# FFN 2's down product as fp32r halves, in the leaky gate's bank, with new orders of the last layers

## What is computed

```python
x = x + L1_ffn(LSTM(x, cond))      # int8-like activations, ternary weights, depthwise conv over time, SiLU
x = x + L2_ffn(RNN(x, cond))
x = x + L3_ffn(leaky(cond, x))

def _L2_ffn_ref(x, W1, b1, W2, b2):
    h = jnp.einsum('bsd,fd->bsf', x, _ternary(W1)) + b1          # 128 -> 512
    h = jax.nn.gelu(h, approximate=False)
    out = jnp.einsum('bsf,df->bsd', h, _ternary(W2)) + b2        # 512 -> 128
    return out

# L3 conditioning, a recurrence over time on the output of layer 2:
gate = jax.nn.sigmoid(h @ Wh.T + z_t @ Wz.T + b)
h_new = jnp.tanh(h * leak + gate * z_t)
```

## Time and profile before

| | |
|---|---|
| Time, median of 3 | 554.75 us (554.6 to 555.09) |
| Profiled execution, its own time | 554.63 us |
| Its span | 553.3 us |
| Granted TensorE clock | 1.0 of full speed |
| PE busy over the span | 540.1 us (98%) |
| DVE busy | 425.7 us (77%) |
| ACT busy | 380.6 us (69%) |
| POOL busy | 197.8 us (36%) |

### The profile page before, as it was taken

How to read it: one execution, slowest core, us unless ns; L and a number is a source line. 1 busy time by engine, 2 the same in 40 slices (tenths; PEclk the granted TensorE clock), 3 DMA queues, 4 the chain that set the end, 5 groups by cost and what they waited for, 6 DMA issues and landing times.

```text
span 553.3 us, 10078 instructions
## 1 busy us (share of the span) xinstructions
PE 540.1 (98%) x3341; PEld 468.0 (85%) x3341; DVE 425.7 (77%) x1026; ACT 380.6 (69%) x857; POOL 197.8 (36%) x186
## 2 busy tenths in 40 slices
PE   8999999999999999999999989999999999999997
PEld 7877888887887899999999877788989999987785
DVE  4987656567659779676856359998999999999866
ACT  4567767758767664454552246888988888888965
POOL 4688788788788402947100000010000000000100
PEclk9999999999999999999999999999999999999999
DMA  8634306512081302021000000122111111112211
GB/s 285 194 152 159 152 1 230 191 56 97 2 305 43 124 10 82 1 73 62 2 1 1 0 1 2 20 39 21 21 20 20 21 31 30 34 38 47 45 52 39
DMA packets 30227, 37.36 MB, mean 68 GB/s; under 512 B 20096, under 2 KB 23648, under 8 KB 29280
## 3 DMA queue, kind: packets, MB, share of 16 engines
q1 hardware_dynamic: 30176, 36.72, 21.2%
HBM read 30.24 MB, written 2.28 MB: 59 GB/s over the span
## 4 chain that ended last, share of the span: by engine, by line
PE 81%; DVE 12%; ACT 4%; issue 2%; POOL 1%; DVEq 0%; ACTq 0%
PE bank L325 11%; PE bank L1248 10%; PE bank L327 10%; PE bank L326 10%; PE bank L1673 4%; PE bank L1759 4%; PE bank L1663 4%; PE bank L1700 3%; PE bank L1701 3%; PE bank L1316 2%; PE bank L1198 1%; PE bank L1748 1%; PE bank L1786 1%; PE bank L409 1%; PE bank L1772 1%
## 5 line engine op out<-in xcount | busy, mean ns | idle before, releaser
L387 POOL TENSOR_TENSOR hidden_low<-hidden,hidden_high 128x512 fp32r<-128x512 f32 x72 | 94.4, 1318 | 24.6 <-ACT hidden_high L372 22.4
L2054 POOL CAST h_high<-h 128x256 fp32r<-128x256 f32 x15 | 6.4, 426 | 197.6 <-ACT h L1865 191.2
L452 ACT ACTIVATE bank<-bank 128x512 f32<-128x512 f32 x56 | 32.6, 583 | 34.5 <-PE bank L327 34.3
L456 DVE TENSOR_TENSOR hidden<-bank,big 128x512 f32<-128x512 f32 x56 | 38.5, 688 | 15.8 <-ACT bank L452 14.6
L372 ACT CAST hidden_high<-hidden 128x512 fp32r<-128x512 f32 x70 | 43.0, 615 | 3.3 <-DVE hidden L456 1.9
L1700 PE MATMUL bank<-taps_high,q1T 128*128 128x512 f32 x94 | 42.9, 457 | 1.0 <-ACT q1T L1828 0.6
L325 PE MATMUL bank<-xin_high,sw_high 128*128 128x256 f32 x128 | 43.9, 343 | 0.0
L1701 PE MATMUL bank<-taps_low,q1T 128*128 128x512 f32 x94 | 37.1, 395 | 0.0
L1382 DVE COPY yT<-bank 128x256 f32<-128x256 f32 x32 | 13.6, 424 | 30.4 <-PE bank L1248 30.4
L1801 ACT ACTIVATE gates_t<-bank,lstm_b_half 128x128 f32<-128x128 f32 x96 | 28.2, 364 | 12.2 <-PE bank L1673 8.8
L1663 PE MATMUL bank<-x,lstm_wx 128*128 128x128 f32 x256 | 34.4, 277 | 1.7 <-ACT gates_t L1801 0.9
(11 more groups left out here) (270 smaller groups left out, 1736.6 us busy)
## 6 DMA issues: line engine op xcount, KB each, us to landing
big<-gates_scratch SPq DMA_DIRECT2D x7, 2048.0 KB, 8.1
w<-in_f_w SPq DMA_DIRECT2D x16, 256.0 KB, 6.2
onehot<-topi_scratch SPq DMA_DIRECT2D x8, 512.0 KB, 4.2
outT<-x SPq DMA_DIRECT2D x15, 128.0 KB, 2.1
xT<-in_xT SPq DMA_DIRECT2D x3, 512.0 KB, 7.4
hidden<-in_ffn_w SPq DMA_DIRECT2D x3, 256.0 KB, 5.2
hidden<-in_conv_w SPq DMA_DIRECT2D x3, 256.0 KB, 4.8
xT<-in_xT SPq DMA_DIRECT2D x2, 256.0 KB, 4.2
```

What stands on the lines that cost most here:

```text
L387: pool.tensor_tensor(hidden_hl[u % 3][1][:, :], hidden[u % 3][:, :], hidden_hl[u % 3][0][:, :].bitcast(F32), ALU.subtract).then_inc(s_lo, 1)
L456: dve.tensor_tensor(hidden[u % 3][:, :].rearrange("p (i k) -> p i k", k=P), r_bank[j % 2][:, :].rearrange("p (i k) -> p i k", k=P), gate_r ...
```

## The change

For blocks 0 to 12 (`SPLIT = 13`) ScalarE copies all 1024 columns of g2 rounded to fp32r (`split_g_high`), GpSimd subtracts that copy from g2 (`split_g_low`), and `down2` multiplies both parts, eight fp32r matmuls in place of four fp32 ones. Both parts have two buffers. The later blocks keep fp32. The down product's bank is now the second half of bank 6, whose first quarter is the leaky gate's; `up2` no longer waits for `new_x3`, `down2` waits for the leaky gate's tanh and for `new_x3` of the block before, and `gelu` waits for the subtraction. ffn2_w2 becomes a fp32r tile beside its raw one. The factor half_ws2 moves from m2w into `new_x2`. The orders of all engines are written anew; in TensorE's loop down2, leaky and mix_products work on blocks one turn older (down2 by two numbers, since it moved from the end of the turn to its start).

```diff
+            SPLIT = 13
             def bank_down(v):
-                return (bank[3] if v <= PAIRS else bank[0])[:, 0:width(v) * P].rearrange("p (s n) -> p s n", s=width(v))
+                dst = bank[6][:, 2 * P:4 * P] if v < PAIRS else (bank[3] if v == PAIRS else bank[0])[:, 0:P]
+                return dst.rearrange("p (s n) -> p s n", s=width(v))
...
             def up2(v, half):
...
                         elif v:
-                            pe.wait_ge(c_x3, v)
+                            pe.wait_ge(c_g2[1], v)
...
             def down2(v):
                 if has_block(v):
-                    pe.wait_ge(c_g2[0], v + 1)
-                    pe.wait_ge(c_g2[1], v + 1)
+                    if v < SPLIT:
+                        pe.wait_ge(c_glow, v + 1)
+                    else:
+                        pe.wait_ge(c_g2[0], v + 1)
+                        pe.wait_ge(c_g2[1], v + 1)
+                    if v == 0:
+                        pe.wait_ge(c_to, EARLY)
+                    elif v < PAIRS:
+                        pe.wait_ge(c_x3, v)
+                        pe.wait_ge(c_g3, 2 * v)
                     for f in range(HT):
-                        mm = pe.matmul(bank_down(v), ffn2_w2[:, f, :], part(g2[:, f, :, :], v),
-                                       start=(f == 0), stop=(f == HT - 1))
+                        if v < SPLIT:
+                            pe.matmul(bank_down(v), ffn2_w2[:, f, :], g2_high[:, v % 2, f, :, :], start=(f == 0), stop=False)
+                            mm = pe.matmul(bank_down(v), ffn2_w2[:, f, :], g2_low[:, v % 2, f, :, :],
+                                           start=False, stop=(f == HT - 1))
+                        else:
+                            mm = pe.matmul(bank_down(v), ffn2_w2[:, f, :].bitcast(F32), part(g2[:, f, :, :], v),
+                                           start=(f == 0), stop=(f == HT - 1))
                     mm.then_inc(c_down, 1)
...
-                    act.activation(ys[:, t % 2, :], ps_y, ACT.Copy, scale=m2w[:, t:t + 1]).then_inc(c_ys, 1)
+                    act.activation(ys[:, t % 2, :], ps_y, ACT.Copy, scale=m2[:, t:t + 1]).then_inc(c_ys, 1)
...
             def gelu(v, half):
                 if has_block(v):
                     act.wait_ge(c_up[half], v + 1)
-                    if v:
+                    if 0 < v <= SPLIT:
+                        act.wait_ge(c_glow, v)
+                    elif v:
                         act.wait_ge(c_down, min(v, PAIRS))
...
+            def split_g_high(v):
+                if 0 <= v < SPLIT:
+                    act.wait_ge(c_g2[0], v + 1)
+                    act.wait_ge(c_g2[1], v + 1)
+                    if v >= 2:
+                        act.wait_ge(c_down, v - 1)
+                    act.copy(g2_high[:, v % 2, :, :, :], g2[:, :, :, :]).then_inc(c_ghigh, 1)
...
-                    dve.tensor_scalar(m2w[:, 2 * p:2 * p + 2], m2[:, 2 * p:2 * p + 2], half_ws2[:, 0:1], None, ALU.mult)
...
-                    dve.tensor_tensor(x1[:, t, :], x1[:, t, :], ps_yT, ALU.add).then_inc(c_x2, 1)
+                    dve.scalar_tensor_tensor(x1[:, t, :], ps_yT, half_ws2[:, 0:1], x1[:, t, :], ALU.mult, ALU.add).then_inc(c_x2, 1)
...
+            def split_g_low(v):
+                if 0 <= v < SPLIT:
+                    pool.wait_ge(c_ghigh, v + 1)
+                    if v >= 2:
+                        pool.wait_ge(c_down, v - 1)
+                    pool.tensor_tensor(g2_low[:, v % 2, :, :, :], g2[:, :, :, :], g2_high[:, v % 2, :, :, :].bitcast(F32),
+                                       ALU.subtract).then_inc(c_glow, 1)
```

More of the change, by code:

```diff
@@ L2212, in pe_program @@
                 up_tap(29, 2)
                 down1(24)
+                turn_q1(30)
+                turn_q1(31)
+                down2(9)
+                turn_y(24)
+                mix_products(7)
                 up_tap(30, 0)
+                up_tap(30, 1)
+                rnn(24)
+                up_tap(30, 2)
                 up2(11, 0)
[L2216 to L2221 removed]
@@ L2222, in pe_program @@
-                up_tap(31, 0)
-                mix_products(8)
-                down1(25)
-                up2(11, 1)
-                up_tap(31, 1)
-                turn_y(25)
+                leaky(18)
+                down1(25)
+                up_tap(31, 0)
+                turn_y(25)
+                up_tap(31, 1)
+                up2(11, 1)
+                rnn(25)
+                leaky(19)
+                down1(26)
+                value(7)
+                down2(10)
+                turn_y(26)
@@ L2236, in pe_program @@
+                leaky(22)
                 mix_products(9)
-                down1(27)
-                leaky(22)
-                turn_y(27)
-                up2(12, 1)
-                rnn(27)
-                value(9)
-                down1(28)
-                leaky(23)
-                down2(12)
-                turn_y(28)
-                mix_products(10)
-                rnn(28)
-                leaky(24)
                 down1(29)
@@ L2626, in dve_program @@
+                conv_next(9)
+                new_h(12)
+                inverse_hs(3)
+                conv_here(9)
+                conv_last(9)
+                new_x2(4)
+                conv_next(10)
+                gate_products(13)
+                new_cell(13)
+                conv_here(10)
+                for q in range(FILL, TURNS):
                     new_h(2 * (q - 2) + 1)
-                    conv_last(2 * (q - 3))
                     silu(q - 4)
                     max_h(q - 2)
-                    leaked3(2 * (q - 8))
+                    conv_last(2 * (q - 3))
+                    gated3(2 * (q - 9))
+                    step_h(q - 2)
+                    leaked3(2 * (q - 9))
+                    result(q - 12)
+                    inverse_h(q - 2)
+                    new_x2(2 * (q - 6) + 1)
+                    gate_products(2 * (q - 1))
@@ L2643, in dve_program @@
-                leaked3(19)
-                conv_last(29)
-                result(6)
-                conv_next(30)
-                conv_here(30)
-                new_x2(24)
-                gated3(20)
-                gated_value(7)
+                    mix(q - 10, xk, mu_k, c_xk)
+                    inverse_hs(q - 4)
+                    mix(q - 10, xr, mu_r, c_xr)
+                    gated_value(q - 11)
+                    gated3(2 * (q - 9) + 1)
+                    new_h(2 * (q - 1))
@@ L2651, in dve_program @@
+                    leaked3(2 * (q - 9) + 1)
+                    conv_here(2 * (q - 3) + 1)
+                    new_x2(2 * (q - 5))
+                    conv_last(2 * (q - 3) + 1)
+                    new_x3(q - 8)
+                    conv_next(2 * (q - 2))
+                    gate_products(2 * (q - 1) + 1)
+                    shift_diff(q - 9)
+                    new_cell(2 * (q - 1) + 1)
+                    conv_here(2 * (q - 2))
+                result(6)
                 conv_last(30)
-                result(7)
@@ L2662, in dve_program @@
+                gated_value(7)
+                new_x3(10)
+                silu(15)
+                max_hs(15)
+                step_hs(15)
+                new_x2(27)
+                inverse_hs(15)
+                gated3(20)
+                leaked3(20)
                 shift_diff(9)
-                leaked3(21)
+                result(7)
                 mix(9, xr, mu_r, c_xr)
                 gated_value(8)
-                new_x2(26)
+                gated3(21)
+                leaked3(21)
```

424 lines of the change are left out of this document (207 added, 217 removed).

## The result

The changed kernel takes 578.87 us (577.34 to 581.18, four runs) against 554.75 before. The ratio is 1.0437, 95% interval 1.0398 to 1.0477: 4.4% slower, where 546.9 was forecast. The profiled execution took 577.34 us, its span is 576.0 us.

The account below looks back on a forecast made before the run. TensorE was taken to bound the loop. 554.63 - 10.3 (down products) - 0.5 (m2w) + 0.9 (ScalarE friction) + 1.2 (depth) + 0.9 (holds in the VectorE-filled stretch) = 546.8, 546.9 us on the median; range 542.5 to 553.0.

Parts of the forecast that it names:

- So I take no new hold in the loop: Steady loop: the GpSimd subtraction holds no further VectorE operation; 0 us taken, bounds 0 and 2.41 a turn.
- The run of five operations: VectorE in the loop: conv_here to conv_next read banks, take 2.57 us, and so cover the 2.41 us subtraction unheld.
- VectorE's own 12.40 us: Steady loop: VectorE's busy time a turn after the change, 12.53 less 0.13 for the dropped m2w.
- the lock: Loop rival: subtraction meets silu, the mix or gate_products, holding VectorE up to 2.41 us; 558.5 to 565.6 us, chance 0.10.
- The down product: TensorE, blocks 0 to 12: 1.73 us becomes 0.94, saving 0.79 a block, 10.3 us in all; loop surcharge only changes place.
- ScalarE: Loop: one copy a block at 0.95 us, ScalarE 12.15 to 12.67 busy a turn; 0.9 us lost in nine turns.
- GpSimd's duration: GpSimd, one 128x1024 subtraction a block: 2.41 us, from a line through its smaller sizes.
- The hold of operations with two SBUF inputs and not of bank reads: VectorE beside a GpSimd subtraction: operations with both inputs in SBUF wait until it ends, those reading a bank do not.
- m2w: VectorE, turns before 377 us: dropping this 0.13 us operation saves 0.5 us, 0.8 at most; hidden in the loop.
- The banks: TensorE's down product in its new bank: the changed waits cost nothing; uncovered, some 0.3 us a turn.
- The orders: End of the kernel: two more leaky steps cost 1.2 us, bounds 2 gained and 6.1 lost; two holds add about 0.9.
- the second rival: End of the kernel: one turn more of depth at full price, 6.1 us in place of 1.2; 551.7 us, chance 0.08.

Follow-up runs that it names:

- experiment 1: Changed kernel, but GpSimd's subtraction waits for leaked3 (blocks 2 to 11) or new_h (block 0): 555.43 us, 1.0005 of the kernel before.
- experiment 8: experiment 1 with the subtraction of blocks 11 and 12 in four pieces of 128x256: 551.80 us, 0.995 of the kernel before.
- experiment 4: Changed kernel with the subtraction cut to 2 columns from block 2 on and down2 of blocks 0 to 12 again four fp32 matmuls: 561.24 us, 1.011.
- experiment 2: Changed kernel, but from block 2 on the subtraction covers 2 of 1024 columns: 551.88 us, 0.994 of the kernel before.
- experiment 5: Kernel before, plus an unneeded 128x1024 GpSimd subtraction behind split_h2 of pairs 1 to 13: 562.46 us, 1.0142.
- experiment 7: Kernel before, plus an unneeded 128x1024 GpSimd subtraction behind split_h2 of pairs 2 to 9, waiting for new_cell of step 2p+11: 566.03 us, 1.021.
- experiment 3: Changed kernel, but every subtraction made in four instructions of 128x256 in place of one of 128x1024: 562.02 us, 1.0124 of the kernel before.
- experiment 10: experiment 8 with the pieces of block 11 also waiting for silu of the last pair: 553.98 us, 0.9983 of the kernel before.

## Why the prediction was wrong

The step that failed is the one on GpSimd's subtraction: "So I take no new hold in the loop". It aligned the subtraction with VectorE's list as if VectorE reached new_h when tanh_cell was done. Tanh_cell ends at 469.9, and new_h is issued at 471.11, since VectorE runs behind ScalarE by the mix, gated_value and a `p` that h_low holds. The subtraction is ready at 471.00. The run of five operations does fit, 2.57 us as worked out, but nothing made the subtraction wait for it. In experiment 1 GpSimd could have begun at 456.51 (h_low's end), while new_h starts at 456.58, leaked3's `pre` at 456.78 and the five operations at 457.04: without the wait the subtraction is ready 0.53 us too early, with two operations of two SBUF inputs still to come. The first of them pays 2.17 us. VectorE's own 12.40 us of the prediction and that hold make 14.57, the turn measured. The rival that is called the lock (the subtraction holds a VectorE operation, for up to its 2.41 us) had the cause and the size of the steady turn (14.0 to 14.8 us; it is 14.57), though it named silu, the mix and gate_products as what would be held and not new_h, with a chance of 0.10 that was far too low. Its time, 558.5 to 565.6 us, still falls 13 us short, and not in the loop: between the profiled executions before and after, 2.4 of the 22.7 us are lost by the fifth tanh_conv, 7.0 in the nine turns to the fourteenth, 5.3 from there to the last and 8.0 behind it, where the rival had a small gain outside the turns. It said itself that VectorE has only 0.2 us of room; that should have been read as a forecast. Experiments 1 and 8 give 23.4 and 3.6 us of the 32.0 between forecast and result to the holds and the half clock that followed them.

Point by point, for the rest:

- The down product: right. The split is worth 0.79 us a block in the loop (experiment 4), and in the chain of experiment 8 it is 0.99, since its first matmul behind down1 takes 0.18 in place of 0.12, a surcharge that the prediction placed there.
- ScalarE: right. The copy takes 0.94 us start to start, the steady turn of experiment 8 has ScalarE 12.34 busy in 12.49, inside the 12.15 to 12.67 worked out. It is no bound, by a hair.
- GpSimd's duration: right, 2.41 forecast, 2.40 measured.
- The hold of operations with two SBUF inputs and not of bank reads, as read from the earlier trace rows: right. hL takes 2.45 us beside a 2.40 us subtraction (0.28 elsewhere), and the tap operations take their usual 0.74 beside one of 2.39 (experiment 1). But the tensor_scalar at 526.59, with one SBUF input, was held as well (2.23 us in place of 0.16). No run shows why; I had looked for two-input operations only.
- m2w: forecast 0.5 us, measured 0 within 0.1%.
- The banks: no wait of them shows; TensorE has no gap in the steady turn of experiments 1, 2 and 8.
- The orders: under-priced. I took 1.2 us for the deeper pipeline and 0.9 for two holds in the end. Without long holds, experiment 8 is 11.0 us ahead of the kernel before at its fourteenth tanh_conv (485.4 against 496.4), 7.6 at its last (504.2 against 511.8) and 3.3 at the end: the stretch after it is 45.84 us against 41.54. Part of that is work that the orders moved there, which I had counted. Experiment 4 puts the price of the orders and the copy at 6.3 us, near the full price of the second rival ("6.1 us in place of 1.2"), which had the depth of the end alone for it; that the two agree is in part luck, since the hold of block 0 is in the 6.3. How it divides between depth, the copy, the hold of block 0 and the half clock at 377 us was not separated.

So 4.9 us are left between the best version (551.80) and the forecast (546.9), and they lie behind the loop, not in it: its steady turn, 12.49 us, is below the 12.6 of the forecast.

## What to carry to other kernels

When work is put on GpSimd beside a busy VectorE, price it by which VectorE operation comes due while it runs: the same subtraction in the kernel before left the turn at 13.35 us at one place (experiment 5) and made it 14.68 at another (experiment 7). And make the program say so: a semaphore that starts the GpSimd instruction behind the last operation that it may not hold (experiment 1, 23.4 us). Where the GpSimd instruction is ready before the last operation that it may hold, as here by 0.5 us, the hold is to be forecast, and here, where VectorE had no idle time in the turn, it was paid in full (12.40 + 2.17 = 14.57 us). Whether it matters that the held operation is in a recurrence was not tested. Where the place can't be had, several short instructions in place of one shorten each hold: in experiment 3 hL took 0.82 us beside pieces of 0.72 to 0.90, in place of 2.45 beside the whole.

## What the runs showed of the hardware that I had not expected

A VectorE tensor_scalar on 2 columns with one SBUF input waited 2.1 us for a GpSimd subtraction (2.23 in place of 0.16). A tensor_reduce with one SBUF input neither held GpSimd nor was slowed by it: in experiment 10 it ran from 508.02 in its usual 1.22 us beside the pieces of the subtraction, four of them in 2.82 us from 508.16. VectorE got in between two instructions of GpSimd's queue (hL 0.82 and `pre` 0.81 us beside pieces of 0.72 to 0.90, experiment 3). And stretches at half the TensorE clock followed short idle times of TensorE: 3.4 us from 376.4 after 1.5 us idle and 3.4 us from 530.0 after 2.0 (the changed kernel), 10.2 us from 507.9, when TensorE was in 2.6 us of idle time until 508.52 (experiment 1, busy 3.37 of 6.00 us), and 3.4 us from 511.7 in experiment 10 after 3.98 of 6.60 us busy. But the clock stayed full after 1.5 us idle until 375.79 in experiment 2, behind the same hold of block 0, and after 1.5 us until 507.54 in experiment 8. So what decides is not shown. It differs between executions of one kernel (the clock is a mean over the whole of each): in one of ten of experiment 10 and two of ten of experiment 1 the mean clock is 1.000, in the others 0.990 to 0.997 and 0.991 to 0.999.
